# Self-attention stage of a one-core decoder layer: quantised keys and values handled inside their accumulator bank, the row normalisation moved behind the score maxima, and the queries signalled in two halves

## What is computed

```python
xn = rms(hidden_states, g1)
q = (xn @ qgroup(w_q).T).reshape(B, S, H, HD).transpose(0, 2, 1, 3)      # 8 heads of 128
k = (xn @ qgroup(w_k).T).reshape(B, S, KVH, HD).transpose(0, 2, 1, 3)    # 2 heads of 128
v = (xn @ qgroup(w_v).T).reshape(B, S, KVH, HD).transpose(0, 2, 1, 3)
k = qgroup(k)                         # 4-bit rounding over each group of 128
q = q * cos + rot_half(q) * sin
k = k * cos + rot_half(k) * sin
...
v = qgroup(v)
scores = jnp.einsum('bhqd,bhkd->bhqk', q, k) / np.float32(np.sqrt(HD))
scores = jnp.where(causal[None, None], scores, NEG)
attn = jax.nn.softmax(scores, axis=-1)
o = jnp.einsum('bhqk,bhkd->bhqd', attn, v).transpose(0, 2, 1, 3).reshape(B, S, H * HD)
h = hidden_states + o @ qgroup(w_o).T
hn = rms(h, g2).reshape(T, D)
logits = hn @ w_gate.T                # then routing to two of eight experts
```

## Time and profile before

| what | value |
|---|---|
| median of 3 runs | 1322.47 us (1319.14 to 1323.29) |
| the profiled execution's own time | 1324.56 us |
| its span in the profile | 1322.8 us |
| instructions | 25732 |
| busy: PE, DVE | 1020.8 us (77%), 1036.9 us (78%) |
| busy: ACT, POOL | 742.8 us (56%), 612.1 us (46%) |
| granted TensorE clock over the span | 0.882 |

### The profile page before, as it was taken

The page is one execution under the profiler, slowest core; times in us unless marked ns, Lnnn a source line. Parts: engine busy times, 40 slices in busy tenths (PEclk is TensorE's granted clock), DMA queues, the critical chain, the costliest instruction groups (busy, mean ns, idle before and its releaser), DMA issues.

```text
span 1322.8 us, 25732 instructions
## 1 busy us (share of the span) xinstructions
PE 1020.8 (77%) x7366; PEld 763.7 (58%) x7367; DVE 1036.9 (78%) x2283; ACT 742.8 (56%) x1866; POOL 612.1 (46%) x805
## 2 busy tenths in 40 slices
PE   0335786763698899996899999982799999999980
PEld 0233342432576777773556666652788888888870
DVE  6893999999889988864788888875577777777765
ACT  4784644430678888871555555541366666666650
POOL 3895787775344444431355544443332233322325
PEclk9755987886789988886899999996899999999995
DMA  5953100003133333312022222221011111111105
GB/s 188 380 194 160 44 0 32 0 32 104 60 119 134 113 108 107 112 37 76 2 84 84 83 83 83 79 77 40 26 37 38 36 40 40 34 36 40 40 27 190
DMA packets 51884, 105.70 MB, mean 80 GB/s; under 512 B 9808, under 2 KB 36432, under 8 KB 51328
## 3 DMA queue, kind: packets, MB, share of 16 engines
q1 hardware_dynamic: 47472, 92.39, 20.0%
q0 software_dynamic: 4368, 12.78, 3.1%
HBM read 73.06 MB, written 32.10 MB: 79 GB/s over the span
## 4 chain that ended last, share of the span: by engine, by line
PE 40%; DVE 25%; issue 13%; POOL 7%; ACT 4%; DMA 1%; DVEq 0%; POOLq 0%; SPq 0%; ACTq 0%
PE banks L1996 14%; PE banks L2006 10%; PE banks L1360 4%; DVE mix_sums L671 4%; POOL whole L1119 2%; DVE carry L661 2%; PE banks L1352 2%; PE banks L1382 2%; ACT whole_level L1047 2%; DVE kvq L1666 2%; DVE carry L658 2%; DVE whole_stat L227 2%; DVE q_rot L1631 1%; DVE top L642 1%; DVE q_sin L1633 1%
## 5 line engine op out<-in xcount | busy, mean ns | idle before, releaser
L2079 DVE SCALAR_TENSOR_TENSOR expert_gate<-banks,expert_steps,expert_chunk 128x128 f32<-128x128 f32 x546 | 166.1, 346 | 96.8 <-ACT expert_chunk L2041 94.8
L1996 PE MATMUL banks<-expert_parts,levels 128*128 128x128 bf16 x3276 | 228.8, 220 | 8.5 <-issue 5.6
L1996 PEld LDWEIGHTS banks<-expert_parts,levels 128*128 x3276 | 202.6, 98 | 49.3 <-issue 21.7
L2006 PE MATMUL banks<-down,up 128*128 x546 | 176.2, 406 | 0.0
L2041 ACT COPY expert_chunk<-banks 128x256 f32<-128x256 f32 x273 | 101.7, 372 | 103.4 <-PE banks L1996 103.4
L2134 POOL DMA_INDIRECT chosen_d<-expert_y,expert_target x39 | 39.0, 999 | 204.0 <-ACT expert_y L2051 204.0
L519 PE MATMUL banks<-x_turned,w_rkv 128*128 128x512 f32 (+1 forms) x192 | 101.7, 690 | 38.9 <-DVE weight L652 38.3
L2045 ACT ACTIVATE silu<-expert_gate,expert_steps 128x128 f32<-128x128 f32 x273 | 110.6, 405 | 16.3 <-DVE expert_gate L2079 16.2
L414 PE MATMUL banks<-consts,level 128*128 128x128 f32 x154 | 35.4, 422 | 87.2 <-POOL level L397 87.2
L2086 DVE SCALAR_TENSOR_TENSOR up<-expert_gate,expert_steps,silu 128x128 f32<-128x128 f32 x273 | 94.4, 346 | 9.3 <-ACT silu L2045 9.3
L1119 POOL TENSOR_TENSOR whole<-whole_level,whole_stat 128x896 bf16<-128x896 f32 x32 | 53.3, 1686 | 102.1 <-DVE whole_level L1188 102.1
(11 more groups left out here) (237 smaller groups left out, 2560.3 us busy)
## 6 DMA issues: line engine op xcount, KB each, us to landing
whole_raw<-in_weight_jobs SPq DMA_DIRECT2D x16, 896.0 KB, 4.9
raw<-in_weight_jobs SPq DMA_DIRECT2D x11, 896.0 KB, 5.7
numbers_d<-turned SPq DMA_DIRECT2D x11, 896.0 KB, 5.1
levels_d<-whole_t SPq DMA_DIRECT2D x16, 448.0 KB, 2.7
levels<-levels_d SPq DMA_DIRECT2D x16, 448.0 KB, 3.6
down<-numbers_d SPq DMA_DIRECT2D x16, 448.0 KB, 4.3
finish_moe<-chosen_d SPq DMA_DIRECT2D x8, 512.0 KB, 7.4
normed_d<-normed_parts SPq DMA_DIRECT2D x16, 192.0 KB, 1.9
```

The lines of the kernel that those rows point to most:

```text
L1996: last = pe.matmul(banks[:, at, (m * DC + c) * ROWS:(m * DC + c + 1) * ROWS], levels[:, bass.ds(expert * (2 * JOB) + (m * JOB + (f * DC + ...
L2006: last = pe.matmul(banks[:, Y + j, 0:D], up[j][:, f, :], down[:, bass.ds(expert * JOB + f * D, D)], start=(f == 0), stop=(f == FC - 1))
L2079: last = dve.scalar_tensor_tensor(out=gate[slot(j, f)][:, m, :], in0=halves(at)[:, m, 1, :], scalar=steps[j][:, m, 1, f:f + 1], in1=chunk[ ...
```

## The change

Four edits, all in `attend_stage`:

1. `project_q` raises `q_ready` behind each of its two halves (four heads, 512 columns each) and not once behind both; `rotate_q(n, m)` waits for its own half.
2. `round_kv` (ACT) writes the rounded keys and values back into their bank, and `kv_scale` (DVE) clips them there, in place; only its last four instructions write `kvq[j]` in SBUF, reading the bank.
3. `x_norm` of a sequence leaves the end of step n and stands in step n + 1 behind `mask_scores`, so behind the peaks. Its `x_stats` stays in step n.
4. `x_stats` comes ahead of `h_norm` at the end of a step.

```diff
@@ project_q (PE)
                 for c in range(DC):
                     last = pe.matmul(banks[:, Q + m, :], xn_t[:, c, :], w_qkv[:, c, 512 * m:512 * m + 512],
                                      start=(c == 0), stop=(c == DC - 1))
-            last.then_inc(s["q_ready"], 1)
+                last.then_inc(s["q_ready"], 1)
@@ round_kv (ACT)
-        def round_kv(j, n):
+        def round_kv(n):
             act.wait_ge(s["kv_scaled"], n + 1)
             for a in range(2 * KVH):
-                last = act.activation(kvq[j][:, a, :], banks[:, KV, a * HD:(a + 1) * HD], ACT.Identity,
+                part = banks[:, KV, a * HD:(a + 1) * HD]
+                last = act.activation(part, part, ACT.Identity,
                                       bias=kv_stat[:, LOW, a:a + 1], scale=kv_stat[:, INV, a:a + 1])
@@ rotate_q (DVE)
         def rotate_q(n, m):
+            dve.wait_ge(s["q_ready"], 2 * n + m + 1)
             if m == 0:
-                dve.wait_ge(s["q_ready"], n + 1)
                 if not (isinstance(n, int) and n == 0):
                     dve.wait_ge(s["q_turned"], 2 * n)
@@ kv_scale (DVE)
-            a, x = kv_stat, kvq[j]
+            a, kv = kv_stat, banks[:, KV, :]
             dve.wait_ge(s["kv_rounded"], n + 1)
             dve.wait_ge(s["kv_scaled"], n + 1)
-            st.did(dve.tensor_scalar(x[:, :, :], x[:, :, :], MAGIC, MAGIC + LEVELS, ALU.max, ALU.min))
+            st.did(dve.tensor_scalar(kv, kv, MAGIC, MAGIC + LEVELS, ALU.max, ALU.min))
             st.wait()
             for g in range(2 * KVH):
-                last = dve.tensor_scalar(x[:, g, :], x[:, g, :], a[:, LOW, g:g + 1], a[:, SCALE, g:g + 1], ALU.subtract, ALU.mult)
+                last = dve.tensor_scalar(kvq[j][:, g, :], banks[:, KV, g * HD:(g + 1) * HD], a[:, LOW, g:g + 1],
+                                         a[:, SCALE, g:g + 1], ALU.subtract, ALU.mult)
             st.did(last)
@@ step (DVE)
         def step(j, n, i, prev, more):
             mask_scores(n)
+            if prev and more >= 2:
+                x_norm(j, n + 2)
             if more:
                 kv_stats(n + 1)
...
             if prev:
                 h_stats(1 - j, n - 1, i)
-                h_norm(1 - j, n - 1)
             if more == 3:
                 x_stats(1 - j, n + 3, i + 2)
-                x_norm(1 - j, n + 3)
+            if prev:
+                h_norm(1 - j, n - 1)
```

More of the change, by code:

```diff
@@ L1513, in step @@
             if more:
-                round_kv(1 - j, n + 1)
+                round_kv(n + 1)
             if more >= 2:
@@ L1528, in scalar @@
         take_x(0)
-        round_kv(0, 0)
+        round_kv(0)
         take_x(1)
```

## The result

The changed kernel takes 1301.02 us (median of 4 runs, 1298.44 to 1303.15) against 1322.88 us before (1319.14 to 1325.26, 4 runs beside them): ratio 0.9836, interval 0.9807 to 0.9866, 21.9 us less. A second set of runs gave 1303.63 against 1321.24, ratio 0.9864 (0.9843 to 0.9884).

A forecast was written before the change was run, and what follows sets the result against it. PE's idle set a 15.71 us step floor; the rebuilt chain through DVE, POOL and PE gave 16.1. 15 seams x 1.0 - 0.2 + 1.7 = 16.5 us gained, median 1306.0 us, range 1302 to 1310, chance 0.47.

The forecast's parts named there:

- The shares: Split of the step's 1.0 us gain: edits 1, 3 and 4 about 0.7, edit 2 about 0.3.
- The step, 16.1: Steady step of the stage: falls from 17.12 to 16.1 us, a gain of 1.0 us.
- for a DVE instruction that gets in ahead: 0.2 us added to the end of POOL's second query rotation, putting `turn_q` at 11.5 us after the mask's start.
- The mask within 0.1 of the scores' end: At the seam: the mask follows the scores by about 0.05 us, not 1.06.
- M + 5.28: Start of the query rotation on DVE, 5.28 us after the mask's start, without waiting for PE.
- M + 10.04: End of the probabilities on POOL, 10.04 us after the mask's start, so PE's 0.84 us wait vanishes.
- `kv_scale`: On DVE: clip in the bank 0.69 us, its four bank-fed instructions 1.15 us, bounds 0.85 and 3.54.
- `rotate_k` would be held up by POOL: Key rotation on DVE: delayed up to 1.3 us, ending at latest 12.4 us after the mask's start; PE asks at 13.0.
- The floor of 15.71: PE in the steady step: no step below 15.71 us, from 17.12 less 1.41 of PE idle.
- rival B: PE alone binds in the stage: 15.71 us a step, 22.9 us gained, time 1299.6 us; chance 0.18.
- The stage's ends: Opening of the stage gains 1.7 us; last seam 0.2 us less to win; nothing behind the stage is touched.

The follow-up runs named there:

- e3: Edits 1, 3 and 4 made on the kernel before, without edit 2: 1309.83 us, ratio 0.9885 to the kernel before, step 16.41 us.
- e9: The changed kernel with value groups scaled behind the key rotation's products: 1301.96 us, ratio 0.9859 to the kernel before, step 15.95 us.
- e1: Edit 2 alone on the kernel before: 1311.2 us, ratio 0.9896 to the kernel before, step 16.28 us.
- e2: Edits 3 and 4 alone on the kernel before: 1321.97 us, ratio 0.998 to the kernel before, step 16.93 us.
- e7: The changed kernel with key groups scaled back into their bank and rotated from there: 1300.61 us, ratio 0.9851 to the kernel before, step 15.76 us.
- e11: The changed kernel without edit 3, `x_norm` back at the step's end behind `h_norm`: 1293.91 us, ratio 0.9777 to the kernel before, step 15.36 us.
- e8: The changed kernel with the key and value projection computed twice: 1323.62 us, ratio 1.0002 to the kernel before, step 16.93 us.
- e10: The changed kernel run again, unaltered: 1303.63 us, ratio 0.9864 to the kernel before, step 15.75 us.

## Why the prediction was right, point by point

- **Direction and mechanism: right; the size a good 5 us short.** 1306.0 was forecast and 1301.02 measured, 1 us outside the forecast's own range of 1302 to 1310. For the stage 16.5 us were forecast and the profiles show 23.2. The difference is 4.8 in the 13 steps between masks 1 and 14, 2.6 in the first step and 0.8 in the last, less 0.4 in the opening and 1.2 behind the last mask.
- **The shares.** They were written as 0.7 for edits 1, 3 and 4 and 0.3 for edit 2. The first was right, 0.71 (e3). The second came out at 0.66, more than double, since the next link was shorter than forecast, as the next point says.
- **The step, 16.1: 0.35 too long.** Two terms of the sum were too large. The 0.2 "for a DVE instruction that gets in ahead" is real (e9) but not due here: `rotate_k` comes at 773.14, when POOL's second rotation has begun. And POOL's multiplication fell from 2.10 to 1.90 (in e1 and in the changed kernel; in e2 and e3, without edit 2, it stays 2.10). In the kernel before it is 1.90 too in the last step, where no `kv_scale` runs beside it. The likely cause is the clip in SBUF that ran beside its start; no run separates it from the four instructions behind it. I had carried the old figure. The other terms differ by 0.17 less (`turn_q` to `turn_k` 1.35 for 1.52) and 0.15 more (`turn_k` to the end of the scores 3.23 for 3.08), which nearly cancel.
- **The mask within 0.1 of the scores' end: right** (776.82 + 2.02 = 778.84, mask 778.88). `x_norm`, forecast near 0.5, takes 0.47. The rotation, forecast at M + 5.28, comes at M + 5.30. The probabilities, forecast at M + 10.04, end at M + 9.86, for the reason above.
- **`kv_scale`: right**, clip 0.69; the four take 1.36 where 1.15 was forecast, and e7 shows that the keys had slack. The forecast that `rotate_k` would be held up by POOL was right too: its first product takes 1.34 for 0.43.
- **The floor of 15.71: wrong.** e11 runs the same PE work at 15.36, and by e8 the floor is at most 15.21. I took PE's idle as 223 less its busy time, but rows that overlap by 0.17 us when PE runs freely hide the short waits: in the changed kernel the rows leave (180 - 177.59) / 11.4 = 0.21 us of idle a step where 1.72 us of added work found 0.54. The Trainium skill warns of this in "Trainium Kernel Development and Optimization", section "Performance Expectations": matmul busy time is a bad measure, since matmuls are pipelined. The trace agrees: the weight loads showed 0.37 and 0.38 us of waiting where the matmul rows showed none. That put rival B's 1299.6 on a false ground, and the measured time near it doesn't make it right: PE alone didn't bind.
- **Edit 3 was credited with a gain that is edit 4's.** The prediction gave both edits the mask right behind the scores. Edit 3 takes `x_norm` from a place before the mask and puts it in the loop; with edit 4 and without edit 3 (e11) the mask follows the scores too, and the step is 0.39 shorter.
- **The stage's ends.** Forecast 1.7 for the opening and 1.0 and 0.8 for the first and last step. The profile shows 1.35, 3.59 and 1.63, in e10 the first step 2.3. `turn_probs` of the first step took 1.97 before, at a granted clock of 0.50 (the 1.2 GHz level), and 1.09 after, at 1.00:

```profile
631.21 1.09 PE L1390 MATMUL banks<-consts,att_probs 128*128 128x128 f32 x8 [1.13 <-POOL att_probs L1579]
```

  Some is given back behind the last mask: the same operation there takes 1.97 after (clock 0.50) and 1.09 before (clock 1.00), and the tail is 25.46 us (857.15 to 882.61) against 24.31. The forecast had no term for either, so what the first step gave beyond 1.0 us was luck. When the granted clock falls in these stretches differs from profile to profile, even of the same kernel (the first step took 15.26 in the changed kernel and 16.56 in e10); why was not tried, and stays open.

## What to carry to other kernels

Draw the loop of waits of one steady step as sums from its start, and ask of each edit whether its instruction lies in the loop or beside it: 1.9 us less in `kv_scale` gave 0.84 alone, because 0.92 of it came back as a wait for POOL; a signal for each half gave 0.33 to 0.53; and a norm that was moved out of a wait into the loop gave away the 0.4 that e11 got back. Test edits that are made together apart as well: of the two at the seam, one did all the good. Where an engine idles just ahead of a wait for another, that is the place for work with nowhere to be. Don't take an engine's busy share for its floor: add work to it and see how much of that the step takes up.

## What the runs showed of the hardware

- A DVE instruction with two SBUF inputs that meets a running POOL operation on SBUF ended 0.28 us behind it (`x_norm` 0.47 to 0.94, first product of the key rotation 0.42 to 1.35). With one input from a bank that product took 0.42 in all 16 sequences (e7).
- The other order was seen as well: in e11 `x_norm` starts 0.07 us ahead of POOL's `add_input` and takes 0.48, while `add_input` takes 0.92 to 1.02 and not 0.72.
- When the first product of the key rotation stood waiting as one POOL operation ended, it went first and POOL's next took 1.45 us and not 1.27 (e9). In the kernel before a `tensor_scalar` of 128 columns stood waiting in that place, and POOL's next took 1.27.
- A 512-column f32 `tensor_scalar` takes 0.41 us in SBUF and 0.69 in its bank. The edit with the slower one was still a gain: the four instructions behind it no longer waited for POOL (3.54 to 1.36), and POOL's multiplication beside them fell from 2.10 to 1.90.
- PE's rows showed 98.7% busy, 0.21 us of idle a step, and work of 0.54 us a step still found room (e8).
